# Unread products on TensorE ahead of two waits of the mixer phase

## The chip, the cores and the metric

The kernel runs on one core of a Trainium2 chip. The metric is the device time of one execution in microseconds (us); lower is better. TensorE does the matrix products (PE in the profile; PEld is its weight load), VectorE (DVE), ScalarE (ACT) and GpSimd (POOL) do the element-wise work, and SyncE (SP) issues the transfers. The engines run their own instruction streams and wait for each other on semaphores.

## The reference

A network of two layers on x of 16 batches x 512 tokens x 128 features in fp32. The lines that matter here are the last three of its six residual steps:

```python
x = x + 0.5 * _L1_ffn_ref(_layernorm(x), gate_w, gate_b, expert_w, expert_b)
x = x + _L1_attn_ref(_layernorm(x), W_in, A_log, dt_bias, B_norm_bias, C_norm_bias, W_out)
x = x + 0.5 * _L1_ffn_ref(_layernorm(x), gate_w, gate_b, expert_w, expert_b)
```

`_L1_ffn_ref` runs all 8 experts on every token, `relu(x @ W_e.T + b_e)`, and sums them with weights that are counted over all tokens of all batches. `_L1_attn_ref` is a state-space mixer: a projection `x @ W_in` to 1056 columns, a scan over chunks in which each chunk makes a state (`einsum` of decay, B and x), the states are carried on with a decay, and the output is a product inside the chunk plus a product with the carried state, then a gate, an rms norm and `@ W_out`.

## The kernel before, in words

The program has three phases, one after the other: `attention_phase` (the first three residual steps), `mixer_phase` (the first expert step and the mixer) and `last_ffn_phase` (the last expert step). The change is in `mixer_phase` alone.

`mixer_phase` is a software pipeline over the 16 batches. In iteration `i` of `ITERATIONS` (19) four stages run side by side, each on a batch of its own: `ffn` on batch i (8 experts, their sum, the norm), `prep` on i - 1 (the projection and all that is made from it), `scan` on i - 2 (the four chunks of the scan) and `tail` on i - 3 (the output product, the norm, the router's gate). All four stages are there in iterations 3 to 15.

Each iteration is a list of slots `q`. The dictionary `MIXER_AT` says by hand in which slot each step stands, and every engine walks the same slots in order, so this table is the order of each engine's instructions. A chunk `t` of the scan has two steps on TensorE. `chunk(b, t)` (L1611) makes the chunk's two half states; VectorE's `states` adds them to what is carried (L1179, L1186). `chunk_rest(b, t)` waits for those states (semaphore `state`), then makes the product inside the chunk (L1625) and the product with the carried states (L1633). For the third chunk, t = 2, `chunk_rest` is in slot 66, and what stands before it in TensorE's order are the products of the last experts, slots 59 and 64 (L1533).

Slot 68 is `sumT`. The experts' sum lies in three parts: `acc` (VectorE) and two of `rl` (ScalarE's relu, L1398, added in pairs by GpSimd, L1486). TensorE waits for `added` (GpSimd), for `xl` of the batch before (the last reader of PSUM bank 2) and for `ex_v` (VectorE), and then adds the three parts and transposes them in one go, 12 products with the identity into bank 2, `ps[:, 2, :]` (L1711). VectorE reads the bank in slot 71 (L1286).

Bank 2 is used by `sumT` in slot 68 and by the transposes of the norm in slot 80 (L1528); the last to read it is VectorE in slot 82, and TensorE waits for that (`xl`) before it projects in slot 1 of the next iteration.

Other steps on TensorE that the prediction names: the output product (L1669, once in an iteration, and so a mark of where an iteration starts), the mean of squares (L1653), the turning of the mixer's output (L1646), and the router's gate in slot 16 (L1678), which waits for a ScalarE copy, `xnT` (L1416).

Of the kernel before, what the change touches and what calls it, by code (L numbers as in the profile page):

```python
# [22 lines left out]
P = 128  # L23
# [918 lines left out]
def mixer_phase(nc, x_in, n_in, x_out, n_out, w, ew, cnt_acc):  # L942
# [4 lines left out]
    with ExitStack() as ctx:  # L947
# [50 lines left out]
        ps = ctx.enter_context(nc.psum_tensor("m_ps", [P, 8, 512], F32))  # L998
# [10 lines left out]
        S = {n: ctx.enter_context(nc.semaphore("m_" + n)) for n in [*PER, "x_in0", "x_in1", "x_out0", "x_out1", "n_in0", "n_in1", "n_out", "dve", "pool", "start", "counted", "weights", "rate"]}  # L1009
# [8 lines left out]
        def upto(name, b, n):  # L1018

            return PER[name] * b + n  # L1020

        def all_of(name, b):
            return PER[name] * (b + 1)

        def batches(i):

            return [b if 0 <= b < BATCH else None for b in (i, i - 1, i - 2, i - 3)]

        with nc.Block(no_gpsimd_drain=True) as block:
# [493 lines left out]
            def _(pe):  # L1523
                mm = nc.tensor.matmul
# [75 lines left out]
                def chunk(b, t):  # L1600
                    par = b % 2
                    hh = M_HEADS // 2

                    pe.wait_ge(S["xv"], upto("xv", b, t + 1))
                    if t or b:
                        pe.wait_ge(S["prod"], upto("prod", b, t))
                    for hf in range(2 if t < NT - 1 else 1):
                        rows = slice(64 * hf, 64 * hf + 64)
                        for r in range(R):
                            for a in range(2):  # L1610
                                ins = mm(ps[64 * a:64 * a + 64, 6 + hf, 384 * hf:384 * hf + P], br[rows, par, t, r, :],  # L1611
                                         xv[rows, t % 2, 2, hh * a:hh * a + hh, r, :],
                                         start=r == 0, stop=r == R - 1, skip_group_check=True)
                        ins.then_inc(S["st_mm"], 1)
                def chunk_rest(b, t):
                    par = b % 2

                    pe.wait_ge(S["state"], upto("state", b, min(2 * t + 2, 2 * NT - 1)))

                    if t == 0:  # L1620
                        pe.wait_ge(S["gs"], all_of("gs", b))
                    for r in range(R):
                        for blk in range(P // BLK):
                            cols = slice(BLK * blk, BLK * blk + BLK)
                            mm(ps[cols, 6, 128:384], gs[:, par, t, r, cols], xv[:, t % 2, blk % 2, :, r, :],  # L1625
                               start=r == 0, stop=r == R - 1, skip_group_check=True)

                    for hf in range(2):
                        k = 2 * t + hf
                        for a in range(2):  # L1630
                            rows = slice(64 * a, 64 * a + 64)
                            held = state[rows, k % 4, :] if k else zero[rows, :]
                            ins = mm(ps[64 * hf:64 * hf + 64, 6 + a, 384 * (1 - a):384 * (1 - a) + P],  # L1633
                                     bt[rows, par, t, 1, 64 * hf:64 * hf + 64], held,
                                     start=True, stop=True, skip_group_check=True)
                    ins.then_inc(S["ymm"], 1)
# [13 lines left out]
                def mean_square(b, t):  # L1650
# [8 lines left out]
                   stop=True).then_inc(S["counted"], 1)  # L1659
                for i in range(ITERATIONS):  # L1660
                    ffn, prep, scan, tail = batches(i)
                    for q in range(SLOTS):
                        if tail is not None:
                            if q == AT["wo"]:
                                pe.wait_ge(S["yz"], all_of("yz", tail))
                                pe.wait_ge(S["ms"], all_of("ms", tail))
                                for t in range(NT):
                                    for c in range(2):
                                        ins = mm(ps[:, 5, P * t:P * t + P], yzT[:, t, c, :], w["w_out"][:, c, :],  # L1669
                                                 start=c == 0, stop=c == 1)  # L1670
                                ins.then_inc(S["wo"], 1)
                            if q == AT["turn_gate"]:
                                pe.wait_ge(S["xn2"], all_of("xn2", tail))
                                transposes(xn[:, 1], 5, S["xT2"])
                            if q == AT["gate"]:
                                pe.wait_ge(S["xnT2"], all_of("xnT2", tail))
                                for t in range(NT):
                                    ins = mm(ps[:, 5, EXPERTS * t:EXPERTS * t + EXPERTS], xnT[:, P * t:P * t + P],  # L1678
                                             w["gwT"][:, :], start=True, stop=True)
                                ins.then_inc(S["gate"], 1)  # L1680
                        if scan is not None:
                            if q in AT["chunks"]:
                                chunk(scan, AT["chunks"].index(q))
                            if q in AT["chunks_rest"]:
                                chunk_rest(scan, AT["chunks_rest"].index(q))
                            if q in AT["mean"]:
                                mean_square(scan, AT["mean"].index(q))
                            if q in AT["turn_y"]:
                                if tail is not None and q == AT["turn_y"][0]:
                                    pe.wait_ge(S["gate_read"], all_of("gate_read", tail))  # L1690
                                turn_y(scan, AT["turn_y"].index(q))
                        if ffn is not None:
                            if q in AT["experts"]:
                                e = AT["experts"].index(q)
                                if e == 0:
                                    pe.wait_ge(S[f"n_in{ffn % 2}"], 16 * (ffn // 2 + 1))
                                    if ffn == 0:
                                        pe.wait_ge(S["weights"], 1)
                                if EXPERTS * ffn + e >= 2:
                                    k = "relu" if e % 2 else "ex_v"  # L1700
                                    pe.wait_ge(S[k], upto(k, ffn, e // 2))
                                three_products(ps[:, e % 2, :], lambda h: ew["hl"][:, h, e, :],
                                               lambda l: xe[:, ffn % 2, l]).then_inc(S["ex"], 1)
                            if q == AT["sumT"]:
                                pe.wait_ge(S["added"], all_of("added", ffn))
                                if ffn:
                                    pe.wait_ge(S["xl"], all_of("xl", ffn - 1))
                                pe.wait_ge(S["ex_v"], all_of("ex_v", ffn))
                                for t in range(NT):
                                    for k, part in enumerate((acc[:, 1], rl[:, 0], rl[:, 2])):  # L1710
                                        ins = mm(ps[:, 2, P * t:P * t + P], part[:, P * t:P * t + P], w["ident"][:, :],  # L1711
                                                 start=k == 0, stop=k == 2)
                                ins.then_inc(S["sumT"], 1)
                            if q == AT["turn2"]:
                                pe.wait_ge(S["xn"], all_of("xn", ffn))
                                transposes(xn[:, 0], 2, S["xT"])
                        if prep is not None:
                            if q in AT["project"]:
                                project(prep, AT["project"].index(q))
                            if q == AT["gates"]:  # L1720
                                gates(prep)
                            if q == AT["sums"]:
                                sums(prep)
                            if q == AT["bt"]:
                                turn_bc(prep)
                            if q == AT["scores"]:
                                scores(prep)
# [259 lines left out]
```

## Time and profile before

| | |
|---|---|
| median of 3 timed runs | 2549.31 us (2544.57, 2549.31, 2550.05) |
| profiled execution, its own time | 2546.41 us |
| its span, first to last instruction | 2544.6 us |
| PE busy in the span | 2163.0 us (85%), 14116 products |
| DVE, ACT, POOL busy | 1832.3 (72%), 1410.1 (55%), 1454.1 us (57%) |
| where the phases change | first product of the mixer phase at 1619.3, of the last phase at 2438.2 us |
| mean granted TensorE clock over the span | 0.946 |

A busy share is an average over the three phases. "PEclk" in a row is the granted TensorE clock as a share of 2.4 GHz: 1.00 is 2.4 GHz, 0.50 is 1.2 GHz. An idle time in square brackets ahead of "<-" is how long the engine stood still before the instruction, and what ended it.

### The profile page before, as it was taken

Reading aid. Unit: us, or ns where it says so; the run is one execution under the profiler, and the core shown is the slowest. Engines: PE = TensorE matmul, PEld = TensorE weight load, DVE = VectorE, ACT = ScalarE, POOL = GpSimd, SP = SyncE. Lnnn points to the kernel's source line nnn. Section 1 sums busy time; section 2 is a strip of 40 time slices with the busy share of each in tenths; the row PEclk is TensorE's granted clock in tenths of the full one; section 3 lists DMA queues with packets and bytes.
Section 4 is the critical chain, followed back from the end, with each engine's and each line's share of the span. In section 5 each row is a group of like instructions: output and inputs, shape, how many; then the busy total and the mean of one; then the engine's idle time right before and its main releaser. Section 6 shows DMA issues by size and latency. Waiting matters only on the chain. (4 is left out here: it accounts for less than half of the span.)

```text
span 2544.6 us, 39733 instructions
## 1 busy us (share of the span) xinstructions
PE 2163.0 (85%) x14116; PEld 1006.0 (40%) x14116; DVE 1832.3 (72%) x4240; ACT 1410.1 (55%) x2651; POOL 1454.1 (57%) x1264
## 2 busy tenths in 40 slices
PE   3689989989989989988988988478888888888778
PEld 1223323323323323333323322246566565665544
DVE  5777777777777776776776772268888887887558
ACT  2166566566566566566566566254655545546235
POOL 3365665665665665665665645145655555555358
PEclk9799999999999999999999999589999999999779
DMA  3221212112112112112112110100000000000033
GB/s 115 54 49 41 48 34 51 43 34 55 38 34 63 30 34 63 30 34 63 36 35 52 42 56 9 33 11 24 26 22 26 22 26 22 23 17 18 10 99 108
DMA packets 86598, 103.70 MB, mean 41 GB/s; under 512 B 10240, under 2 KB 68736, under 8 KB 86272
## 3 DMA queue, kind: packets, MB, share of 16 engines
q1 hardware_dynamic: 86400, 101.16, 15.1%
q8 instruction: 113, 1.85, 0.3%
q14 instruction: 85, 0.70, 0.1%
HBM read 29.55 MB, written 20.97 MB: 20 GB/s over the span
## 5 line engine op out<-in xcount | busy, mean ns | idle before, releaser
L347 DVE TENSOR_REDUCE mS<-ps 128x1 f32<-128x512 f32 x1024 | 676.2, 680 | 303.2 <-PE ps L724 298.8
L506 ACT ACTIVATE pr<-ps 128x512 f32<-128x512 f32 x1024 | 585.7, 597 | 382.9 <-PE ps L708 365.5
L579 POOL TENSOR_TENSOR prs<-pr 128x512 f32<-128x512 f32 x384 | 487.4, 1288 | 243.7 <-ACT pr L506 243.7
L708 PE MATMUL ps<-qst,kst 97*128 97x512 f16 x1024 | 397.5, 391 | 53.2 <-ACT pr L506 52.1
L724 PE MATMUL ps<-kst,qst 96*128 96x512 f16 x1024 | 401.4, 393 | 36.6 <-DVE mS L347 25.5
L746 PE MATMUL ps<-pr,vt 128*32 128x512 f32 x2048 | 279.3, 618 | 0.0
L708 PEld LDWEIGHTS ps<-qst,kst 97*128 97x128 f16 x1024 | 99.0, 98 | 418.1 <-ACT pr L506 307.7
L583 POOL TENSOR_TENSOR terms<-terms 128x512 f32<-128x512 f32 x128 | 162.5, 1270 | 68.8 <-DVE terms L340 68.8
L340 DVE TENSOR_TENSOR terms<-ps,shared 128x512 f32<-128x512 f32 x256 | 172.8, 677 | 34.9 <-POOL lo L588 28.1
L588 POOL TENSOR_TENSOR lo<-terms,hi 128x512 f16<-128x512 f32 x128 | 148.0, 1157 | 76.9 <-ACT hi L486 76.9
L724 PEld LDWEIGHTS ps<-kst,qst 96*128 96x128 f16 x1024 | 101.2, 99 | 151.0 <-DVE mS L347 81.0
L486 ACT CAST hi<-terms 128x512 f16<-128x512 f32 x128 | 78.8, 616 | 113.3 <-POOL terms L583 113.3
L755 PE MATMUL ps<-prs,ones 128*32 128x512 f32 x768 | 107.3, 632 | 33.7 <-POOL prs L579 33.7
L1394 ACT ACTIVATE m_sqy<-m_yzT 128x256 f32<-128x256 f32 x64 | 26.5, 414 | 191.9 <-DVE m_yzT L1205 191.9
L665 PE MATMUL ps<-xnh,wq 128*128 128x512 f16 x256 | 99.6, 393 | 30.5 <-DVE terms L340 21.6
L1491 POOL TENSOR_TENSOR m_own<-m_own 128x256 f32<-128x256 f32 x64 | 78.5, 1227 | 78.6 <-ACT m_own L1372 78.6
L1164 DVE TENSOR_TENSOR m_xv<-m_xr,m_coef 128x1536 f32<-128x1536 f32 x64 | 118.5, 1854 | 0.0
L1533 PE MATMUL m_ps<-m_xe,ew_hl 128*128 128x512 f16 x384 | 106.1, 397 | 9.7 <-DVE ew_hl L1240 4.2
L1486 POOL TENSOR_TENSOR m_rl<-m_rl 128x512 f32<-128x512 f32 x32 | 60.3, 1886 | 92.9 <-ACT m_rl L1398 92.9
L563 POOL TENSOR_TENSOR rstd<-veps,minus_half 128x8 f32<-128x8 f32 (+1 forms) x38 | 55.1, 1450 | 96.5 <-DVE veps L313 96.5
L665 PE MATMUL ps<-xnh,wk 128*128 128x512 f16 x256 | 97.2, 382 | 12.4 <-DVE terms L340 12.4
L1625 PE MATMUL m_ps<-m_xv,m_gs 128*32 128x256 f32 x1024 | 74.3, 411 | 36.5 <-DVE m_state L1186 36.4
(265 smaller groups left out, 4381.8 us busy)
## 6 DMA issues: line engine op xcount, KB each, us to landing
qst<-hi SPq DMA_DIRECT2D x128, 128.0 KB, 2.3
kst<-hi SPq DMA_DIRECT2D x128, 128.0 KB, 2.4
qst<-lo SPq DMA_DIRECT2D x64, 128.0 KB, 2.3
kst<-lo SPq DMA_DIRECT2D x64, 128.0 KB, 2.4
x<-in_q SPq DMA_DIRECT2D x16, 256.0 KB, 2.8
shared<-in_rope SPq DMA_DIRECT2D x1, 4096.0 KB, 14.5
x<-yold SPq DMA_DIRECT2D x16, 256.0 KB, 2.5
n<-kept SPq DMA_DIRECT2D x16, 256.0 KB, 2.1
```

What stands on the lines that cost most here:

```text
L340: v.tensor_tensor(terms[:, p % 2, c, :], ps[:, 4 + c, :], w["rope"][:, 2 * kq + c, g, :], ALU.mult).then_inc(S["pair_free"], 1)
L347: v.tensor_reduce(mS[:, b % 2, t, s:s + 1], ps[:, 2 + n % 2, :], AX, ALU.max).then_inc(S["s_read"], 1)
L506: a.activation(pr[:, s % 2, g, :], ps[:, g % 2, :], ACT.Exp, scale=ATT_SCALE).then_inc(S["exp"], 1)
L579: g.tensor_tensor(prs[:, c, :], pr[:, 0, c, :], pr[:, 1, c, :], ALU.add).then_inc(S["prs"], 1)
L583: g.tensor_tensor(terms[:, p % 2, 0, :], terms[:, p % 2, 0, :], terms[:, p % 2, 1, :], ALU.add).then_inc(S["rot"], 1)
L588: g.tensor_tensor(lo[:, p // NG, p % NG, :], terms[:, p % 2, 0, :], hi[:, p // NG, p % NG, :], ALU.subtract).then_inc(S["lo"], 1)
L665: ins = mm(out, lhs[a], rhs[b], start=k == 0, stop=k == 2)
L708: mm(ps[:, g % 2, :], kst[:, h, P * kt:P * kt + P], qst[:, h, :], start=True, stop=True).then_inc(S["st"], 1)
L724: mm(ps[:, 2 + n % 2, :], qst[0:3 * DH, h, P * t:P * t + P], kst[0:3 * DH, h, :], start=True, stop=True).then_inc(S["s"], 1)
L746: ins = mm(ps[DH * g:DH * g + DH, 6, :], vt[:, kt, DH * h:DH * h + DH], pr[:, s % 2, g, :], start=kt == 0, stop=kt == NT - 1, skip_group_c ...
L755: ins = mm(ps[DH * g:DH * g + DH, 7, :], w["ones"][:, 0:DH], prs[:, g, :], start=n % 2 == 0, stop=n % 2 == 1, skip_group_check=True)
L1164: v.tensor_tensor(xv[:, t % 2].rearrange("p c h r q -> p c h (r q)"), xr[:, b % 2, t].rearrange("p (o h) r q -> p o h (r q)", o=1).to_broa ...
```

## The change

A helper on TensorE multiplies a piece of the projection's weights with another piece of them (128x128 by 128x512, fp16) into PSUM bank 2. Nobody reads the result, and no semaphore is raised. It is called with 5 in `chunk_rest` ahead of the wait for the third chunk's states, for all 16 batches, and with 2 ahead of the wait for `added` in `sumT`, for all batches but the first. In `sumT` the wait for `xl` now stands first and the wait for `added` behind the two products.

```diff
+                def keep_busy(n):
+                    for _ in range(n):
+                        mm(ps[:, 2, :], w["w_in_hl"][:, 0, 0:P], w["w_in_hl"][:, 0, 0:512], start=True, stop=True)
+
                 def chunk_rest(b, t):
                     par = b % 2
+                    if t == 2:
+                        keep_busy(5)
 
                     pe.wait_ge(S["state"], upto("state", b, min(2 * t + 2, 2 * NT - 1)))
...
                             if q == AT["sumT"]:
-                                pe.wait_ge(S["added"], all_of("added", ffn))
                                 if ffn:
                                     pe.wait_ge(S["xl"], all_of("xl", ffn - 1))
+                                    keep_busy(2)
+                                pe.wait_ge(S["added"], all_of("added", ffn))
                                 pe.wait_ge(S["ex_v"], all_of("ex_v", ffn))
```

## Rows read from the trace of the kernel before

**Rows 1.** The page: busy time of each engine, and PEclk in 40 slices.
```profile
PE 2163.0 (85%) x14116; PEld 1006.0 (40%) x14116; DVE 1832.3 (72%) x4240; ACT 1410.1 (55%) x2651; POOL 1454.1 (57%) x1264
...
PEclk9799999999999999999999999589999999999779
```
**Rows 2.** Windows (stretch, length, busy us per engine, PEclk), from one L1669 to the next.
```profile
1734.97:1780.45 45.48, 39.43 (x379) 27.18 (x379) 37.56 (x102) 25.25 (x52) 26.92 (x25) 1.00 0.08 24
...
1825.92:1872.48 46.56, 40.74 (x379) 28.57 (x379) 37.53 (x102) 25.27 (x52) 26.88 (x25) 0.96 0.08 24
1872.48:1918.26 45.78, 39.43 (x379) 27.18 (x379) 37.63 (x102) 25.25 (x52) 26.90 (x25) 1.00 0.08 25
1918.26:1965.26 47.00, 40.99 (x378) 27.51 (x379) 37.84 (x102) 25.26 (x52) 26.91 (x25) 0.96 0.08 24
1965.26:2012.05 46.79, 40.98 (x379) 28.81 (x379) 38.65 (x102) 25.27 (x52) 26.75 (x25) 0.96 0.08 24
...
2242.01:2288.72 46.71, 40.91 (x379) 28.73 (x379) 38.66 (x102) 25.25 (x52) 26.75 (x25) 0.96 0.04 13
```
**Rows 3.** Waits of TensorE from 1650 to 2350 us: total, times, longest.
```profile
PE m_ps L1625 <- DVE m_state L1186: 25.9, 14, 1.9
PE m_ps L1678 <- ACT m_xnT L1416: 14.3, 14, 1.7
PE m_ps L1711 <- POOL m_rl L1486: 12.0, 14, 3.9
```
**Rows 4.** Windows just before a fall of the clock, and in the fall.
```profile
1715.00:1718.40 3.40, 1.46 (x19) 0.57 (x18) 3.16 (x11) 3.37 (x9) 0.00 (x0) 1.00 0.22 77
1718.40:1725.20 6.80, 6.80 (x42) 5.92 (x35) 5.73 (x7) 0.43 (x1) 6.06 (x6) 0.50 0.00 0
...
1930.00:1933.40 3.40, 2.43 (x29) 1.61 (x29) 1.83 (x6) 3.37 (x6) 3.19 (x2) 1.00 0.07 26
1933.50:1936.80 3.30, 3.30 (x27) 1.06 (x25) 2.79 (x17) 2.59 (x4) 2.27 (x2) 0.50 0.11 41
1994.90:1998.20 3.30, 2.03 (x29) 1.19 (x29) 3.11 (x7) 1.85 (x5) 1.36 (x2) 1.00 0.25 75
1998.40:2001.70 3.30, 3.30 (x17) 3.30 (x17) 2.62 (x3) 0.00 (x0) 3.14 (x3) 0.50 0.00 0
```
**Rows 5.** Timeline of TensorE around both waits, in an iteration at full clock.
```profile
1761.94 1.47 PE L1533 MATMUL m_ps<-m_xe,ew_hl 128*128 128x512 f16 x6
1765.26 1.07 PE L1625 MATMUL m_ps<-m_xv,m_gs 128*32 128x256 f32 x16 [1.85 <-DVE m_state L1186]
1766.26 0.45 PE L1633 MATMUL m_ps<-m_state,m_bt 64*64 64x128 f32 x8
1766.64 0.61 PE L1653 MATMUL m_ps<-m_ones,m_sqy 128*128 128x2 f32 x4
1767.87 0.49 PE L1711 MATMUL m_ps<-shared,m_acc 128*128 128x128 f32 x2 [0.62 <-POOL m_rl L1486]
```
**Rows 6.** Timeline of DVE, ACT and POOL: what ends the two waits.
```profile
1763.74 0.29 DVE L823 TENSOR_SCALAR m_ang<-m_ang 128x256 f32<-128x256 f32 x1
...
1764.92 0.29 DVE L1186 TENSOR_TENSOR m_state<-m_kept,m_ps 128x128 f32<-128x128 f32 x1
...
1765.80 0.67 ACT L1398 ACTIVATE m_rl<-m_ps,posb 128x512 f32<-128x512 f32 x1
...
1766.55 1.26 POOL L1486 TENSOR_TENSOR m_rl<-m_rl 128x512 f32<-128x512 f32 x1 [4.60 <-ACT m_rl L1398]
```
**Rows 7.** Timeline of TensorE: the same products, three at 1.00, six at 0.50.
```profile
1760.59 0.81 PE L1533 MATMUL m_ps<-m_xe,ew_hl 128*128 128x512 f16 x3
...
1664.65 2.74 PE L1533 MATMUL m_ps<-m_xe,ew_hl 128*128 128x512 f16 x6 [3.74 <-ACT m_rl L1398]
```
**Rows 8.** Timeline of TensorE: the first iteration with a scan and a sum.
```profile
1717.71 1.31 PE L1625 MATMUL m_ps<-m_xv,m_gs 128*32 128x256 f32 x16 [1.94 <-DVE m_state L1186]
...
1734.97 2.02 PE L1669 MATMUL m_ps<-shared,m_yzT 128*128 128x128 f32 x16 [0.35 <-DVE m_ms L1210]
```
**Rows 9.** Timeline and windows of TensorE in the last two scans.
```profile
2364.49 1.94 PE L1625 MATMUL m_ps<-m_xv,m_gs 128*32 128x256 f32 x16 [4.27 <-DVE m_state L1186]
...
2406.53 1.07 PE L1625 MATMUL m_ps<-m_xv,m_gs 128*32 128x256 f32 x16 [2.36 <-DVE m_state L1186]
...
2408.00:2421.50 13.50, 12.08 (x68) 9.49 (x68) 2.62 (x6) 0.83 (x2) 0.00 (x0) 0.50 0.01 1
2421.87 3.50 PE L1669 MATMUL m_ps<-shared,m_yzT 128*128 128x128 f32 x16 [0.34 <-DVE m_ms L1210]
```

## The prediction

> **What bounds the kernel now.** I read the page first: PE is busy for 85% of the span, more than any other engine, and PEclk is below 9 in few of the 40 slices [rows 1]. The change is in the mixer phase, so I cut that phase at L1669, once per iteration [rows 2]. The reader is to see that iterations come in two lengths: 45.47 to 45.48 us wherever PEclk is 1.00, apart from one of 45.78 right behind a slower one, and 46.56 to 47.00 us where it is 0.96. DVE, ACT and POOL do the same work in both kinds to within 1.2 us, so it is TensorE's clock that makes the difference. PE is busy 39.43 of 45.48 us: it bounds most of the iteration, and some 6 us are waits.
>
> Then I asked what TensorE waits for [rows 3]. Three of the waits matter. The third chunk's product (L1625) waits for VectorE's states, 25.9 us in 14 iterations, 1.85 us each. The router's gate (L1678) waits for ScalarE, about 1.0 us each. The experts' sum (L1711) waits for GpSimd, 12.0 us with one of 3.9 from the fill of the pipeline, so about 0.6 each. Last I put windows around the places where the clock went from 2.4 to 1.2 GHz [rows 4]. Each fall between iterations 3 and 15 lasts 3.3 to 3.4 us. There are seven falls in the stretch from 1715 to 2334 us: six come right behind the wait for the states (1718.4, 1858.4, 1998.4, 2090.5, 2182.7 and 2274.8 us, the first twice as long), one behind the gate's wait (1933.5 us). What the engine did before them is in the same rows: it was busy for 1.46 and 2.03 of 3.3 to 3.4 us, and part of that with products of 64 or 32 columns, which use a part of the array (L1625, L1633) [rows 5]. In the iterations at full clock the same wait of 1.85 us stands, without a fall. So the wait does not always lose the clock: it does where it falls badly against the moments at which the clock is set, and these moments shift against the iteration.
>
> **The change, part by part.** *Five products ahead of the states' wait.* They are 16 x 5 = 80 products, 128 x 128 by 128 x 512 in fp16, the form of L1533. Three of those take 0.81 us and six 1.47 us, so one more costs 0.66 / 3 = 0.22 us at full clock [rows 5, 7]. At half clock six take 2.74, one more about 0.43. Five cost 5 x 0.22 = 1.1 us and stand in a wait of 1.85 us: TensorE is free at about 1763.4 (end of L1533) [rows 5] and the states are written at 1765.2 by a VectorE chain that works without a pause from the angles (L823) to L1186 [rows 6]. Nothing in that chain waits for these products: all that VectorE needs of TensorE stands ahead of them. The cost is nothing, with 0.7 us to spare. At half clock they take 2.15 us, 0.3 more than the wait. If the cover were gone altogether, they would cost 16 x 1.1 = 17.6 us.
>
> *Two products ahead of the wait for the sum.* 15 x 2 = 30 products, 0.44 us against an idle time of 0.62 [rows 5]. The wait ends with GpSimd's addition, which starts at 1766.55, when ScalarE's relu has ended, and takes 1.26 us [rows 6]; ScalarE was late by its own queue, not by TensorE. Hidden, with 0.18 us to spare; uncovered 15 x 0.44 = 6.6 us. Where the clock is low they show in full: in the first fall there was no wait at the sum at all. The wait for `xl` that now stands first was passed in slot 1 already. The wait for `added` is moved behind the two products, and no DMA and no other queue is moved.
>
> *The clock.* This is where the gain must come from. With the products TensorE works 1.1 of the 1.85 us and 0.44 of the 0.62 us with the full array. Of 2.5 us of idle time 0.9 are left, in two pieces, less than the gate's wait of 1.0 us, which cost the clock only once in thirteen iterations. So I take all six falls away. Their price: the first, 2.07 us (from L1625 to L1669 it is 1734.97 - 1717.71 = 17.26 us [rows 8], where the iteration at full clock has 1780.45 - 1765.26 = 15.19 us [rows 2, 5]). The other five by the lengths in rows 2 against 45.48: 46.56 and the 45.78 behind it, 1.38 us; and four iterations, 46.79, 46.79, 46.74 and 46.71 (first and last are shown), 1.31 + 1.31 + 1.26 + 1.23. Sum 2.07 + 6.49 = 8.6 us.
>
> *What is late next: the gate's wait.* It is not filled. It now makes one fall, 47.00 - 45.48 = 1.5 us. When the iterations no longer stretch, their place against the falls changes, and it can catch more or none. From none (1.5 less) to one in every second iteration, as the states' wait has now from 1998 us on, six in all (5 x 1.5 = 7.6 more). I take two falls, 1.5 us more, nearer to the one of thirteen that is seen.
>
> *The last two scans* [rows 9]. In the first the wait is 4.27 us; 1.1 us of products leaves over 3 us idle, and I take nothing. In the last the wait is 2.36 us, and behind it 12.08 us of work stand at half clock up to L1669. At full clock that is at most 6 us less, at least nothing. I take 2 us, because part of the stretch is waiting for others.
>
> The sum for the profiled execution: - 8.6 + 1.5 - 2.0 = - 9.1, from 2546.4 to 2537.3 us. Its own time is 2.9 us below the median of the runs, which is worth two more falls. On the median that is 2540.2; a part of its two more falls should go too, and I take 0.7 for them: **2539.5 us**.
>
> A rule of the Trainium skill speaks against this. TensorE: Matmul & The Clock Gate, section "HAM oscillation — how this bites in real kernels", explains a lost clock by TensorE idling through a wait for a DMA, which in its kernel is 3 to 5 us long, and asks for no longer gaps. By that rule waits of 1.85 and 0.62 us are harmless, filling them brings nothing, and the time stays at 2549. The trace disagrees: at 1718.4 the clock falls behind a wait of 1.94 us, with no longer one near.
>
> **The rivals.** (A) The forecast. (B) The falls move to the gate's wait, which nothing fills: for it speaks that it is there in every iteration with 1.0 us, against it that it cost the clock once in thirteen. Six falls there: 2549.3 - 8.6 - 2.0 + 7.6 = 2546.3 us. (C) The clock does not count products that fill a short wait, or the falls have another cause: nothing gained, nothing lost, 2549.3 us. (D) Half of it: 0.75 and 0.18 us of idle time are left and still cost half of the falls: 2549.3 - 4.3 = 2545. (E) Slower: the products are on TensorE's path. The place is the sum's wait with its 0.18 us to spare, and the states' wait at half clock. If the drain of the products and the release behind them cost more than these margins, say 0.5 us in each of 15 iterations, and no fall is saved, it is 2549.3 + 7.5 = 2556.8. It decides from 0.6 us per iteration even with the falls saved. Against it: both waits are ended by engines whose chains don't touch TensorE's new products.
>
> **How the numbers follow.** A 0.68, B 0.09, C 0.08, D 0.09, E 0.06. A itself spans 2533 (no gate fall, the last scan at full clock) to 2544. B and D reach to 2547, so the range is 2533 to 2547, and C and E are what is left out. A measurement of this kernel can tell about 0.2% (5.1 us) from no change: below 2544.2 lies nearly all of A and half of D, 0.72; within, the rest of D, B, C, 0.22; slower 0.06.
>
> **What would show it.** In the profile after, right: iterations of 45.5 us almost throughout, with no PEclk of 0.50 behind L1625 of the third chunk; the rest of the wait there 0.7 us and at L1711 0.2 us; the falls that remain stand behind L1678. Wrong: full-clock iterations longer than 45.48 us (E), L1711 no longer waiting for GpSimd and L1286 late (E), falls at the old place with the products in it (C, D), or every second iteration 47.0 us with the fall at the gate (B).

## The result and the profile after

| | before | after |
|---|---|---|
| median of the timed runs, us | 2549.68 (4 runs, 2544.57 to 2552.90) | 2526.60 (4 runs, 2522.40 to 2532.04) |
| ratio after / before | | 0.9925, 95% interval 0.9897 to 0.9952 |
| profiled execution, us | 2546.41 | 2526.62 |

The change makes the kernel faster, by 19 us by the ratio (the ratios and their intervals here are estimates over all runs of both kernels and not quotients of the medians, which would give 23 us). I had forecast 9.8 us and a range down to 2533. The direction and the mechanism were right, the size was not.

The page of the changed kernel, lines to set against [rows 1]: PE is as busy as before, with 110 more products. PEclk looks almost the same, since a 9 stands for anything from 90% on; a change of a few hundredths has to be read from windows.

```profile
PE 2163.5 (86%) x14226; PEld 994.3 (39%) x14226; DVE 1827.8 (72%) x4240; ACT 1410.7 (56%) x2651; POOL 1455.5 (58%) x1264
...
PEclk9799999999999999999999999689999999999789
```

The windows of the changed kernel from one output product (now L1677) to the next, the first two, the fourth and the thirteenth of the iterations with all four stages, and then the two last scans. Columns as in [rows 2].

```profile
1728.94:1774.44 45.50, 40.97 (x386) 27.72 (x386) 37.57 (x102) 25.28 (x52) 26.90 (x25) 1.00 0.08 24
1774.44:1819.93 45.49, 40.96 (x386) 27.71 (x386) 37.57 (x102) 25.25 (x52) 26.91 (x25) 1.00 0.08 24
...
1865.43:1911.24 45.81, 40.96 (x386) 27.72 (x386) 37.66 (x102) 25.27 (x52) 26.92 (x25) 1.00 0.08 25
...
2275.20:2320.68 45.48, 40.96 (x386) 27.72 (x386) 37.56 (x102) 25.26 (x52) 26.91 (x25) 1.00 0.04 13
2320.68:2366.86 46.18, 37.74 (x331) 26.60 (x332) 31.84 (x88) 21.33 (x44) 21.38 (x20) 0.85 0.04 13
2366.86:2404.23 37.37, 29.80 (x250) 20.85 (x250) 19.46 (x56) 6.09 (x15) 11.84 (x13) 0.73 0.05 15
```

There is no fall of the clock left in thirteen iterations. Each takes 45.5 us though TensorE works 1.5 us more in it (40.97 against 39.43): the seven products are hidden. One iteration, the fourth, takes 45.81 us at full clock.

The timeline of TensorE around the two waits, against [rows 5], and the waits, against [rows 3]. L1619 are the new products; L1633 is the old L1625, L1720 the old L1711, L1686 the old L1678.

```profile
1755.93 1.47 PE L1533 MATMUL m_ps<-m_xe,ew_hl 128*128 128x512 f16 x6
1757.23 1.24 PE L1619 MATMUL m_ps<-w_in_hl 128*128 128x512 f16 x5
1759.24 1.07 PE L1633 MATMUL m_ps<-m_xv,m_gs 128*32 128x256 f32 x16 [0.76 <-DVE m_state L1186]
1760.24 0.45 PE L1641 MATMUL m_ps<-m_state,m_bt 64*64 64x128 f32 x8
1760.62 0.61 PE L1661 MATMUL m_ps<-m_ones,m_sqy 128*128 128x2 f32 x4
1761.08 0.59 PE L1619 MATMUL m_ps<-w_in_hl 128*128 128x512 f16 x2
1761.86 0.49 PE L1720 MATMUL m_ps<-shared,m_acc 128*128 128x128 f32 x2 [0.18 <-POOL m_rl L1486]
```

```profile
PE m_ps L1686 <- ACT m_xnT L1416: 14.3, 14, 1.7
PE m_ps L1633 <- DVE m_state L1186: 10.8, 14, 0.9
...
PE m_ps L1720 <- POOL m_rl L1486: 5.6, 14, 3.4
```

What is left of the waits is 0.76 and 0.18 us, as forecast (0.7 and 0.18). L1633 still starts 15.2 us ahead of the next output product. Where the time went, by the starts of the mixer's first product, of the output products and of the last phase's first:

| stretch | before | after | difference | forecast |
|---|---|---|---|---|
| attention phase | 1619.31 | 1618.87 | -0.4 | 0 |
| filling, to the first output product | 115.67 | 110.08 | -5.6 | -2.1 |
| thirteen iterations | 599.22 | 591.74 | -7.5 | -5.0 |
| last two scans to the mixer's last product | 100.87 | 95.26 | -5.6 | -2.0 |
| the rest | 109.57 | 108.91 | -0.7 | 0 |

### The profile page after: what moved, and what is told of

The parts are those of the page before. It is cut to its first block and busy times, and to the rows that moved or that the text cites. A ratio compares the mean times of both kernels' runs of the same rounds, so it can differ in the third digit from the quotient of the medians.

```text
span 2524.8 us, 39953 instructions
## 1 busy us (share of the span) xinstructions
PE 2163.5 (86%) x14226; PEld 994.3 (39%) x14226; DVE 1827.8 (72%) x4240; ACT 1410.7 (56%) x2651; POOL 1455.5 (58%) x1264
## 3 DMA queue, kind: packets, MB, share of 16 engines
q8 instruction: 113, 1.85, 0.3%
## 5 line engine op out<-in xcount | busy, mean ns | idle before, releaser
L571 POOL TENSOR_TENSOR xn<-sq 128x256 f32<-128x256 f32 x64 | 46.7, 749 | 100.4 <-ACT sq L478 100.3
```

## The experiments

The kernels of a series ran on one chip and share its runs of before. The series ran on different chips. The "filling" is the stretch from the mixer phase's first product to the first output product, when the stages start one after another; "the thirteen iterations" are those with all four stages.

**Parts of the change.** E1 is the changed kernel again; in the others one thing is taken away from it.

```diff
# E2: the two products at the sum are left out
-                                    keep_busy(2)
# E3: the five at the states are left out
-                    if t == 2:
-                        keep_busy(5)
# E4: 8 columns instead of 512
-                        mm(ps[:, 2, :], w["w_in_hl"][:, 0, 0:P], w["w_in_hl"][:, 0, 0:512], start=True, stop=True)
+                        mm(ps[:, 2, 0:8], w["w_in_hl"][:, 0, 0:P], w["w_in_hl"][:, 0, 0:8], start=True, stop=True)
```

> The changed kernel again, as the measure for the others of this series. Theory (the clock): the time comes from falls of TensorE's clock that the products prevent, so the ratio is again 0.990 to 0.995, no fall between iterations 3 and 15 stands behind the wait for the third chunk's states, and such an iteration takes 45.5 us. Rival (chance): a good part of the 19.8 us between the two profiled executions came from where the falls of the filling happened to lie; then this time the filling (first product of the mixer to the first output product, 115.67 us before, 110.08 after) is again near 115 and the ratio nearer to 0.996.

> Only the five products ahead of the states' wait; the two ahead of the sum are left out. If the five do the work: at most 2 us slower than both, the steady iterations at 45.5 us, the rest of the wait at the sum 0.6 us. If both waits must be filled, because they lie close together: some of the six falls between 1715 and 2334 us come back, 1.1 to 2 us each, and half of the gain of those iterations (3 to 4 us) is lost.

> Only the two products ahead of the sum; the five are left out. Clock theory: the 1.85 us wait for the states stays empty, the falls behind it come back in about every second iteration, and the time is within 5 us of before (ratio 0.998 to 1.000). The rival that the sum's wait matters alone: as fast as both.

> The same 110 products in the same places, each with 8 columns in place of 512, so the instructions, the order and the moved wait are the same and the array has almost nothing to do. Clock theory: no gain, ratio 0.998 to 1.001, the falls are back. Rival (something other than the array's work: the moved wait, the presence of instructions that keep the queue busy): as fast as both, ratio 0.990 to 0.995.

| | median, us | runs | ratio to before (2546.86, 20 runs) | 95% interval |
|---|---|---|---|---|
| E1 both | 2529.14 | 6 | 0.9932 | 0.9919 to 0.9945 |
| E2 five | 2536.25 | 6 | 0.9958 | 0.9946 to 0.9971 |
| E3 two | 2542.60 | 9 | 0.9978 | 0.9967 to 0.9990 |
| E4 narrow | 2546.83 | 11 | 1.0004 | 0.9994 to 1.0015 |

E4 rules out that the moved wait, or the mere presence of more instructions, brings the gain. It has the same instructions in the same order, and the moved wait, and gains nothing. The timeline at the wait of its first four-stage iteration, then the windows ahead of and in the fall behind it:

```profile
1760.23 0.27 PE L1619 MATMUL m_ps<-w_in_hl 128*128 128x8 f16 x5
1762.24 1.07 PE L1633 MATMUL m_ps<-m_xv,m_gs 128*32 128x256 f32 x16 [1.73 <-DVE m_state L1186]
```

```profile
1760.50:1763.80 3.30, 1.57 (x27) 0.81 (x26) 3.01 (x10) 2.95 (x5) 0.27 (x1) 1.00 0.28 79
1764.00:1770.70 6.70, 6.33 (x31) 6.24 (x32) 4.77 (x6) 0.00 (x0) 6.46 (x7) 0.50 0.01 2
```

The wait is 1.73 us long again and the clock is at half for 6.8 us from 1764 on. The products must do some work: five with 8 columns keep TensorE busy for 0.27 us, five with 512 columns for 1.24 us. (E4 changes the busy time and the width together, so it doesn't tell which of them the clock answers to.) The rule that I had cited against the change (the Trainium skill, TensorE: Matmul & The Clock Gate, "HAM oscillation — how this bites in real kernels") blames waits for a DMA of 3 to 5 us; by it E1 and E4 would both have stayed at before. E1's 17 us against E4's nothing contradict that: waits of 1.85 and 0.62 us cost the clock here.

E2 and E3 show that each group of products brings a part of the gain and that both are needed for the whole. The gains are 10.7 (five) and 5.6 us (two), 16.3 together, and 17.3 for both: to within the intervals the two simply add. E2 was 7 us behind E1, where I had expected to lose 3 to 4 us if both waits matter; E3's ratio of 0.9978 is just outside the 0.998 to 1.000 that I had expected. (E1's filling took 110.3 us, so the rival that gave it 115 fails for this run.) E3's profile has three falls in the thirteen iterations and not one in every second, as I had expected: one behind the gate's wait (1840.9 us) and two behind the empty wait for the states (1950.1 and 2271.0 us), both 6.8 us long. The iteration and the fall of the first of the two:

```profile
1918.73:1966.69 47.96, 42.76 (x381) 30.15 (x381) 37.45 (x102) 25.26 (x52) 26.76 (x25) 0.93 0.08 23
...
1950.20:1956.90 6.70, 6.70 (x36) 6.01 (x33) 4.73 (x6) 0.04 (x1) 6.34 (x7) 0.50 0.01 2
```

E2's profile has four falls in the thirteen iterations, one behind the gate's wait (1793 us) and three at the start of the sum. Here are the windows of two such iterations, and the timeline at the first of these falls:

```profile
1825.11:1871.92 46.81, 42.02 (x383) 29.30 (x384) 38.67 (x102) 25.26 (x52) 26.74 (x25) 0.96 0.07 24
...
2282.80:2329.50 46.70, 41.91 (x384) 29.19 (x384) 37.58 (x102) 25.26 (x52) 26.90 (x25) 0.96 0.04 12
```

```profile
1855.40 1.07 PE L1633 MATMUL m_ps<-m_xv,m_gs 128*32 128x256 f32 x16 [0.77 <-DVE m_state L1186]
1856.40 0.45 PE L1641 MATMUL m_ps<-m_state,m_bt 64*64 64x128 f32 x8
1856.79 0.61 PE L1661 MATMUL m_ps<-m_ones,m_sqy 128*128 128x2 f32 x4
1858.06 0.72 PE L1719 MATMUL m_ps<-shared,m_acc 128*128 128x128 f32 x2 [0.67 <-issue]
1858.57 1.06 PE L1719 MATMUL m_ps<-shared,m_rl 128*128 128x128 f32 x4
```

With the five products in place the clock still falls at 1858.1 us, in the sum's empty wait. Between the end of the five products and this fall (3.5 us) TensorE is idle for 0.77 us at the states and for 0.67 us at the sum; the changed kernel, with both filled, has no fall in any of 39 such iterations (three profiles). I read this as one thin stretch with two waits in it, of which the second still decides when the first is filled. That is a reading of three falls. The prediction had priced both waits as one idle time of 2.5 us, and had no price for either alone.

**Where the gain is.** E5 has the products only in iterations 3 to 15, E6 only in the others. E7 and E8 add to the change.

```diff
# E5 (E6: "not 1 <= b <= 13" and "ffn < 3")
+                    if t == 2 and 1 <= b <= 13:
+                        keep_busy(5)
...
+                                    if ffn >= 3:
+                                        keep_busy(2)
# E7: ahead of the wait for xnT2 at the gate
+                                keep_busy(3)
# E8
+                    if t == 2:
+                        keep_busy(15 if b == 14 else 8 if b == 15 else 5)
+                    if t == 0 and b == 15:
+                        keep_busy(12)
...
+                                    keep_busy(14 if ffn == 1 else 2)
...
+                for _ in range(10):   # last phase, ahead of its wait for the weights
+                    mm(ps[:, 0, :], w["w_in_hl"][:, 0, 0:P], w["w_in_hl"][:, 0, 0:512], start=True, stop=True)
```

> The products only in iterations 3 to 15, where all four stages are there (five for the scans of batches 1 to 13, two for the sums of batches 3 to 15). In the first series the whole change was worth 17.3 us (ratio 0.9932). Theory: the typical run of before loses more in these iterations than the profiled one did (the profile of the kernel with narrow products lost 12 us there, that of before 8), so most of the gain is here: 9 to 12 us, ratio 0.995 to 0.9965, the thirteen iterations in 591.7 us, the filling between 114 and 116 us. Rival: the filling and the last scans carry it, as the two profiled executions say (5.6 and 5.6 of 19.8 us): then 7 us or less are here.

> The complement: products only in iterations 1 and 2 and in the two last scans (16 and 17). Theory: the filling keeps the 2 us fall at its one wait and a little more, the last scans give 0 to 3 us: 4 to 8 us in all, ratio 0.997 to 0.9985. Rival that the last scans' 5.6 us in the first pair of profiles are the change's: 9 to 11 us here, ratio 0.9958 to 0.9965, and the stretch from the fourteenth output product to the end of the mixer 5 us shorter than the 100.87 of before.

> The changed kernel with three more products ahead of the router gate's wait, 0.65 us in an idle time of 0.97 us. My prediction held that the falls would now go to this wait. The two profiles of the changed kernel show none there between iterations 3 and 15, but the last four-stage iteration's successor falls behind it. If typical runs do lose falls there (theory that the spread of the changed kernel, 2522 to 2532, is this): 1 to 4 us faster than the changed kernel, ratio to before 0.9915 to 0.993. If not: the same as the changed kernel, 0.9932, or up to 0.5 us slower.

> The changed kernel with its products dosed to the longer waits at the edges: 14 instead of 2 ahead of the second sum (3.4 to 3.9 us of wait), 15 instead of 5 ahead of the states of the 15th scan (3.1 to 4.3 us), 12 ahead of the first chunk (3.4 us) and 8 ahead of the third of the last scan, and 10 ahead of the last phase's wait for its weights (4.95 us). If a wait's fall can be kept away by filling it, the 10 to 20 us at half clock in the last scans and the 5 us at half clock at the start of the last phase go: 4 to 8 us faster than the changed kernel, ratio to before 0.990 to 0.9917. Rival: these stretches are bound by the chain through VectorE and ScalarE, and the clock does not matter there: 0 to 1 us.

| | median, us | runs | ratio to before (2559.46, 12 runs) | 95% interval |
|---|---|---|---|---|
| E5 steady | 2536.50 | 6 | 0.9915 | 0.9882 to 0.9948 |
| E6 ends | 2534.82 | 7 | 0.9918 | 0.9886 to 0.9950 |
| E7 gate | 2520.64 | 6 | 0.9853 | 0.9819 to 0.9887 |
| E8 edges | 2522.63 | 6 | 0.9858 | 0.9825 to 0.9892 |

The twelve runs of before lay in two groups in this series, five from 2544.7 to 2546.4 and seven from 2557.9 to 2567.2, so the size of the gain depends on the group that one compares with. Against all twelve, by the ratios, E5 and E6 gain some 21 us each. Against the lower group's mean (2545.4) E5 gains 8.9 and E6 10.6 us. The two sum to 19, about the gain of the whole change elsewhere, but the choice of that group is mine. By it E5 is at the lower edge of the 9 to 12 us that I expected, and E6 above its 4 to 8. E5 and E6 differ by less than 2 us: the ends are worth about as much as the thirteen iterations, whichever group one takes, so the rival for E6 fits its time better than the theory did.

E5's profile has one fall in thirteen iterations, behind the gate: the windows of the iteration and of the fall.

```profile
1962.84:2009.86 47.02, 42.53 (x385) 28.02 (x386) 37.85 (x102) 25.25 (x52) 26.91 (x25) 0.96 0.08 24
1978.00:1981.20 3.20, 3.20 (x24) 0.86 (x25) 2.84 (x17) 2.68 (x4) 2.36 (x2) 0.50 0.16 60
```

The kernel lost 593.2 - 591.7 = 1.5 us there, and its filling took 115.6 us, as expected. So the gate's wait can make a fall with the products in place, and it costs 47.02 - 45.50 = 1.5 us, my price. E7 fills this wait. Its thirteen iterations take 591.7 us, as without the gate's products. In its profile the two last scans take 43.53 and 33.26 us, against 46.18 and 37.37 of the changed kernel.

```profile
2326.35:2369.88 43.53, 35.57 (x334) 24.73 (x335) 33.15 (x88) 21.32 (x44) 21.70 (x20) 0.92 0.04 14
2369.88:2403.14 33.26, 24.52 (x252) 16.86 (x253) 19.39 (x56) 6.09 (x15) 11.84 (x13) 0.90 0.05 17
```

That these 6.8 us are the gate products' is not shown. E8, which has more products ahead of the states' wait there and none at the gate, takes nearly the same time for the first of the two scans:

```profile
2323.48:2367.23 43.75, 37.20 (x341) 25.99 (x342) 33.16 (x88) 21.31 (x44) 21.72 (x20) 0.92 0.04 13
```

Against E1's 2529.14 and the changed kernel's 2526.60 us E7 is 6.0 to 8.5 and E8 4.0 to 6.5 us faster, but these are medians from other chips. For E7 I had expected 1 to 4 us, and falls saved inside the thirteen iterations, where its profile shows none saved. E8 takes the last phase from 105.74 to 103.90 us: with its products ahead of the wait the clock is back at full at 2424.4 us, before the first expert product (2425.7), while in the changed kernel it comes back at 2427.5, behind the first (2424.7).

**The change again, all additions, and before again.** E10 is E7 and E8 together. E11 and E12 are the kernel before, unchanged, for two more profiles.

```diff
# E10: the edits of E7 and of E8
# E9: none (the changed kernel); E11, E12: none (the kernel before)
```

> The changed kernel once more, since the last series had no run of it beside the parts and its runs of before lay in two groups (2544.7 to 2546.4 and 2557.9 to 2567.2). Theory: the changed kernel is near 2529 wherever it runs, thirteen iterations in 591.7 us, and the ratio varies between 0.990 and 0.9935 with the runs of before it is compared with. Rival: the changed kernel has a second group too, 12 us or more above the first.

> The changed kernel with both additions, three products ahead of the gate's wait and the doses at the edges. If they act apart, their gains over the changed kernel (about 8 and 6 us by the medians of the two series, on different chips) add up in part: 8 to 12 us faster than the changed kernel in this series. If both live from the same falls in the last scans: no faster than the gate alone, 6 to 8 us.

> The kernel before, for one more profile of it. My sum used one execution, 8.05 us lost to the clock in the thirteen iterations. If that one was milder than usual: here more, 9 to 13 us (600.2 to 604.2 us for the thirteen). If it was typical: 7 to 9 us. An execution of the group above 2557 should show where it loses its 12 us: in the attention phase (the mixer's first product later than at 1619 us) or in the mixer.

> The same once more: a third profile of the kernel before, for the same question and with the same numbers expected.

E9: median 2526.68 us of 6 runs, ratio 0.9923 (0.9897 to 0.9948) to 2547.57 us of before. Five lie from 2522.15 to 2531.48; one took 5175 us, for which I have no explanation (it is in the median and not in the ratio). The changed kernel showed no second group. E10: 2521.88 us, 2517.15 to 2523.38, ratio 0.9906 (0.9885 to 0.9927): 4.8 us faster than E9 by the medians, less than the 6 to 12 expected, and the intervals of the ratios overlap. It is the fastest version that was run beside the changed kernel. E11 took 2541.11 and E12 2544.47 us, with 599.3 and 603.5 us for the thirteen iterations: one answers "typical", the other "milder than usual".

The windows of E12, the kernel before in another execution: the first six four-stage iterations, its filling, and a fall in the filling.

```profile
1728.96:1776.91 47.95, 42.33 (x378) 30.16 (x379) 37.74 (x102) 25.26 (x52) 26.76 (x25) 0.93 0.08 23
1776.91:1824.78 47.87, 42.40 (x378) 30.22 (x379) 37.76 (x102) 25.25 (x52) 26.76 (x25) 0.93 0.08 23
1824.78:1872.61 47.83, 42.40 (x378) 30.23 (x379) 37.74 (x102) 25.25 (x52) 26.77 (x25) 0.93 0.08 23
1872.61:1918.42 45.81, 39.43 (x379) 27.18 (x379) 37.67 (x102) 25.26 (x52) 26.93 (x25) 1.00 0.08 25
...
1963.92:2010.51 46.59, 40.77 (x378) 28.58 (x379) 37.57 (x102) 25.27 (x52) 26.90 (x25) 0.96 0.08 24
...
1614.43:1728.96 114.53, 82.17 (x538) 50.52 (x539) 64.79 (x145) 50.65 (x94) 43.62 (x38) 0.79 0.08 24
1668.80:1675.50 6.70, 4.90 (x23) 4.90 (x24) 3.69 (x5) 0.32 (x1) 5.67 (x5) 0.50 0.02 7
```

This execution loses 2.4 us in each of the first three iterations, since the falls there are twice as long (6.8 us), and 1.1 to 1.2 us in four later ones. The same program takes two courses in the profiles, then, and they part before the filling ends. In course A the clock falls for 3.4 us 17 us after the mixer's first product; in course B the first fall comes 23.5 us after it and lasts 10.2 us. The fourteen profiles of this case:

| | filling | thirteen iterations |
|---|---|---|
| A, before (the first profile and E11) | 115.7, 115.7 | 599.2, 599.3 |
| A, no five products in the filling (E3, E5) | 115.9, 115.6 | 598.1, 593.2 |
| A, with them (E2, E6, E7, E8) | 113.5, 113.5, 113.6, 113.0 | 596.9, 600.3, 591.7, 591.6 |
| B, before (E12), and E4 | 114.5, 114.2 | 603.5, 603.4 |
| B, the changed kernel (after, E1, E9), and E10 | 110.1, 110.3, 110.4, 110.3 | 591.7, 591.6, 591.9, 591.8 |

E6 has no products in the thirteen iterations, and E2 and E3 have one of the two groups. With both waits filled the thirteen iterations take 591.6 to 591.9 us in either course, apart from E5 with its fall at the gate. That fall goes with the course: of the seven profiles of A with an unfilled gate's wait six have one of it in the thirteen iterations (not E8), of the five of B none. The change does not fix the course: before its first new product, at 1671 us, it runs what the kernel before runs; before was seen in both, and E7 and E8, which have all of the change, in A. But all three profiles of the changed kernel are B, and I can't exclude that something in it favours this course. My forecast compared A with A. The profile of after was a B. And the course alone doesn't set an execution's time: the mixer's first product starts anywhere from 1614.4 to 1621.1 us in the fourteen profiles, before anything that the change touches, and so E12 (B) took 2 us less than the first profile of before (A).

## Why the prediction was wrong

In the profiled pair the forecast was 9.1 us and 19.8 were measured. The 10.7 us between them lie in the filling (3.5), the thirteen iterations (2.5), the last two scans (3.6), the rest (0.7) and the attention phase (0.4).

The steps that held. The bound (TensorE's clock makes the two lengths of an iteration) held: in E4 the falls and the longer iterations come back together. The cost of the products, nothing, held: 45.50 us with them, 45.48 without. The price of the falls was right where like is compared with like: course A loses 599.2 - 591.7 = 7.5 us in the thirteen iterations, where I had counted 6.5 behind this wait and 1.5 at the gate's; and the first fall, 2.07 us by my count, is 115.7 - 113.5 = 2.2 us in A. Rival E (the products on the path), B (the falls move to the gate), C and D (half of the falls left) are out.

The steps that failed:

1. "Its own time is 2.9 us below the median of the runs, which is worth two more falls ... I take 0.7 for them." I took one execution for the kernel. In course B the thirteen iterations lose 603.4 - 591.7 = 11.7 us, 4.2 more than in A, and the filling 114.4 - 110.3 = 4.1 us, 1.9 more. The filling's extra fall stands behind the second sum; it is in both B profiles without full products (1668.7 us in E12, 1671.7 in E4) and in none of the three of the changed kernel. In course A two products don't prevent the fall there (E3), fourteen do (E8), but the next fall is then 10.2 us long in place of 6.8 and the filling gains only 0.5 us. I had not counted that wait at all. The profile of after is a B, so the 5.6 us of the filling in the pair hold this term. How often each course comes in the timed runs is not known.
2. The last two scans, "at most 6 us less, at least nothing ... I take 2 us". The first pair of profiles shows 5.6. But this stretch varies without the change: without full products there it took 100.87, 95.55 and 100.39 us in the three profiles of before, 98.16 in E3, 95.56 in E4 and 99.69 in E5, on average 98.4. In the changed kernel it took 95.26, 95.26 and 94.23, on average 94.9, and in E2 and E6, which have the same products there, 96.62 each. The change is worth 2.8 us (by all five) to 3.5 (by the three) of the 5.6, with few samples. The term was too small by some 0.8 to 1.5 us, inside its bounds.
3. "I take two falls, 1.5 us more" at the gate. In three profiles of the changed kernel there is none in the thirteen iterations, so the term should have been about -1.5 instead of +1.5, 3 us. For course A, from which I forecast, it stays between -1.5 and 0: E8 has no fall there and E5 one. Rival B named the right place, as E5 shows, with a frequency that never came. That the iterations no longer stretch, and so do not bring the wait to the same place again, is my reading; no run tests it. After the thirteen, where the gate's wait is 1.72 us long, the clock falls behind it in all three profiles of the changed kernel (at 2335.3, 2331.1 and 2336.5 us, for 6.8 us); in E7, with the wait filled, and in E8, without, it falls there for 3.4 us.
4. The rest, 0.5 us: 109.5 on average of the six profiles without full products in the last scans, 109.0 in the changed kernel. I had not priced it, and no run shows its cause.
5. A small one: I read the 45.78 us behind a slow iteration as the rest of a fall. The fourth iteration takes 45.8 us in every profile, with and without falls, also at full clock after (45.81 above). The fall at 1858 us had cost 1.1 us and not 1.4.

Course A gives 2.2 + 7.5 + 2.8 to 3.5 + 0.5 = 13.0 to 13.7 us, course B 4.1 + 11.7 + 2.8 to 3.5 + 0.5 = 19.1 to 19.8; the ratios of E1 and E9 give 17 and 20. That would fit a mixture, mostly B, but it is not shown, and there are more courses than these two: the granted clock of the 20 runs of before in the first series goes from 0.938 to 0.949, seven of them below the 0.943 to 0.946 of the three profiles. My 9.8 was low even for A, by steps 2, 3 and 4.

What stays open: the group of seven runs of before at 2557.9 to 2567.2 us in one series. Their granted clock was 0.928 to 0.939, where the other five had 0.941 to 0.948, so more of their span was at half clock: on average 338 us and not 279. At 2.4 us for 6.8 us of fall, as in E12's first iterations, the 59 us more would cost 21 us by estimate; the groups' means are 17 apart. None of the kernels with products had such a run, and no profile fell into it, so I can't say in which phase it lies.

## What to carry to other kernels

When the clock falls behind a wait in some iterations and not in others, one profile gives one course of several: take two or three of the kernel before, or bound the term with the densest falls that the trace shows anywhere. Here unread products of 128x128 by 512 columns, dosed to end before the wait does, cost 0.02 us of a 45.48 us iteration and kept the clock; the same number with 8 columns gained nothing (ratio 1.0004). Where two short waits lie close together, fill both: here one alone brought 10.7 us, the other alone 5.6, both 17.3.

## What the runs showed of the hardware

Waits of TensorE of under 2 us can cost it the full clock: at 1718.4 us in the kernel before it falls behind one of 1.94 us, with no longer one near, and filling such waits took the falls away (none in the thirteen iterations of the changed kernel, three profiles). How long PE is shown busy does not tell by itself whether they do. In the kernel before, the 3.4 us up to 1933.4 us have PE busy for 2.43 us, and the clock falls behind them [rows 4]; the 3.4 us up to 1766.2 us, with the same states' wait of 1.85 us in them, have 1.55 us and no fall follows. In E2 the 28 products between the five full ones and the fall at 1858.1 us keep PE busy for 2.0 of 3.5 us, and the clock falls all the same. What else decides, the size of the products or their place, these runs don't part. And the falls repeat: once every second iteration is lengthened by one, as from 1998 us on in the kernel before, the next comes at the same wait two iterations later (46.79, 46.79, 46.74, 46.71 us), up to the end of the thirteen iterations, in all three profiles of before.
